# First attention: one VectorE instruction for two heads' maxima from four PSUM banks, and a scores' ring of two banks

## The chip, the cores and the metric

The kernel runs on one core of a Trainium2 chip. The metric is the device time of one execution in microseconds (us), the median of several. TensorE (PE) multiplies, its weight loader is listed apart (PEld); VectorE is DVE, ScalarE is ACT, GpSimd is POOL, and SyncE (SP) issues most of the DMAs. Results of TensorE go to PSUM, which has eight banks of 2 KB per partition; a bank holds 512 numbers of f32.

## What is computed

Two transformer layers over 2048 tokens of width 512: an attention with 16 heads of 32, a mixture of experts, an attention with one head of 512, and a gated MLP, each with a layer norm behind it. The change lies in the first attention:

```python
q = jnp.concatenate([q_sem, q_geo], axis=-1)
k = jnp.concatenate([k_sem, k_geo], axis=-1)
scores = jnp.einsum('bhqd,bhkd->bhqk', q, k).astype(jnp.float32) * scale
causal = jnp.tril(jnp.ones((S, S), dtype=bool))
scores = jnp.where(causal, scores, jnp.finfo(jnp.float32).min)
attn = jax.nn.softmax(scores, axis=-1).astype(v.dtype)
out = jnp.einsum('bhqk,bhkd->bhqd', attn, v)
```

## The kernel before

The program is a row of stages. `layer0_attention` is the second, after `layer0_qkv`, and all engines pass a border before the third (`layer0_project`) begins. In the trace it lies between about 152 and 731 us.

It works on 16 **items**, each one chunk c of 512 queries (c = 0 to 3) for a group of four heads. Items 0 to 3 have c = 0, items 4 to 7 c = 1, and so on. An item has 4(c+1) **steps**, one for each tile of 128 keys: 4 steps in each of items 0 to 3, 8 in 4 to 7, 12 in 8 to 11, 16 in 12 to 15, 160 in all. Scores are computed twice:

- **Maxima.** A softmax needs a maximum per query. For it TensorE multiplies 128 queries by up to 512 keys (line 866, a **unit**; 16(c+1) units in an item) into `sbank`, three banks used in turn (the **maxima's ring**). Most units are full, 128x512, and VectorE takes their maximum with one `reduce_max` (line 789, 384 of them). Units on the diagonal are 128 to 512 wide and go through an add with a mask and a maximum in one custom instruction (line 794, 256 of them). Heads are the innermost index: head 0, 1, 2, 3 of a query tile follow each other. When an item's maxima are complete, a **turn** transposes them on TensorE (line 873) into a bank of the same ring; ScalarE copies it out (line 758), and DMAs bring it into a row of the queries' tile. Units belong to an item some steps ahead of the one whose steps run.
- **Steps.** TensorE multiplies 128 keys by 512 queries, with the negated maximum as one more row (line 898; 895 and 900 at the diagonal), for each of four heads into `stb`, three banks used in turn (the **scores' ring**). ScalarE takes the exponential of each into `probs`, which has five slots (line 752). TensorE multiplies by the values (line 914), one step behind. GpSimd adds up the probabilities of four steps, in place, three adds in two halves each (line 711), and TensorE sums over the keys of that (line 930); VectorE turns and inverts it (lines 819 to 828), GpSimd multiplies (line 726).

The order of all this is one list (`attention0_plan`), and each engine runs through the list and takes its own events. In a step it reads: scores of head 0, units, head 1, units, head 2, units, values of the step before, sums if due, head 3, units. Mostly one unit stands behind each product of scores; in item 15, the last, none does. Before a unit, `free` waits until the bank's former content was reduced (`unit_max`); before a product of scores, TensorE waits until ScalarE is through with the product three before (`exp_ok`). TensorE, VectorE and ScalarE each take their work strictly in the list's order.

Of the kernel before, what the change touches and what calls it, by code (L numbers as in the profile page):

```python
# [18 lines left out]
ACT = mybir.ActivationFunctionType  # L19
AX = mybir.AxisListType.X  # L20
# [559 lines left out]
def layer0_attention(nc, stage_before, stored, landed, qx, qk_dram, m_dram, xs_dram, acc_dram, token, V, X, hi, lo, fifth, qst, consts, early, out_w, first_o):  # L580
    items, steps, first, final, units, loads, last_use, order = attention0_plan()
    unit_no, ring, scored = {}, {}, {}
    for at, ev in enumerate(order):
        if ev[0] == "unit":
            unit_no[ev] = len(unit_no)
        if ev[0] in ("unit", "turn"):
            ring[ev] = len(ring)
        if ev[0] == "scores":
            scored[ev[1], ev[2]] = at
    on_ring = sorted(ring, key=ring.get)  # L590
# [9 lines left out]
    with ExitStack() as ctx:  # L600
# [18 lines left out]
        stb = m.ps("stb", [P, 3, CH])  # L619
        sbank = m.ps("sbank", [P, 3, CH])  # L620
# [110 lines left out]
        def _(act):  # L731
            for ev in order:
                if ev[0] == "scores":
# [14 lines left out]
                    if per == 1:  # L748
                        to, got = probs[i % PSLOTS][:, h, w0:], stb[:, k % 3, w0:]
                    else:  # L750
                        to, got = probs[i % PSLOTS][:, h + 1 - per:h + 1, w0:], stb[:, k % 3, :].rearrange("p (h n) -> p h n", h=per)
                    nc.scalar.activation(to, got, ACT.Exp, scale=SCALE0).then_inc(s["exp_ok"], 1)  # L752
                elif ev[0] == "turn":
# [4 lines left out]
                    nc.scalar.activation(msb[:, n % 2, :], sbank[0:GH * TC, ring[ev] % 3, 0:P], ACT.Copy)\  # L758
# [78 lines left out]
        def _(pe):  # L837
            def free(ev):

                r = ring[ev]  # L840
                if r >= 3:
                    old = on_ring[r - 3]
                    if old[0] == "unit":
                        pe.wait_ge(s["unit_max"], unit_no[old] + 1)
                    else:
                        pe.wait_ge(s["mcopy"], old[1] + 1)
                return sbank[:, r % 3, :]

            fresh_q, fresh_k = set(range(EARLY)), set(range(EARLY))
            for ev in order:  # L850
# [23 lines left out]
                elif ev[0] == "scores":  # L874
# [10 lines left out]
                    if k >= 3 and j == 0:  # L885
                        pe.wait_ge(s["exp_ok"], k - 2)
# [3 lines left out]
                    if per > 1 and j == 0:  # L890
                        nc.tensor.matmul(stb[:, k % 3, :].rearrange("p (h n) -> p h n", h=per), identr[:],
                                         maskr[:, 0:wide].unsqueeze(1).broadcast_to([P, per, wide]), start=True, stop=False,
                                         skip_group_check=True)
                    if per > 1:
                        last = nc.tensor.matmul(stb[:, k % 3, j * wide:(j + 1) * wide], keys, asked, start=False, stop=j == per - 1,
                                                skip_group_check=True)
                    else:
                        last = nc.tensor.matmul(stb[:, k % 3, w0:], keys, asked, start=True, stop=kt < TC * c)  # L898
                        if kt >= TC * c:
                            last = nc.tensor.matmul(stb[:, k % 3, w0:w0 + P], identr[:], maskr[:, 0:P], start=False, stop=True)  # L900
# [1766 lines left out]
```

## Time and profile before

| | us |
|---|---|
| median of 3 runs | 2221.56 |
| the 3 runs | 2220.63, 2221.56, 2225.43 |
| the profiled execution | 2230.52 |
| its span, first to last instruction | 2228.7 |
| first attention, first unit to last sum, about | 152 to 731 |

The profile is of one execution, 9 us above the median. Its page gives busy times for each engine; stretches of the span can be asked for one by one. Two things need care. A busy PE is not a PE at its peak, since the records of neighbouring matmuls overlap: a product of 512 columns has a record of 0.40 us, and they start 0.235 us apart when nothing holds them. And a matmul that waits has its wait on the weight load in front of it, so a wait for a bank shows in the rows of PEld.

### The profile page before, as it was taken

What the parts mean: (1) busy time and instruction counts of PE and PEld (TensorE: products, weight loads), DVE (VectorE), ACT (ScalarE), POOL (GpSimd) and SP (SyncE); (2) the same over time, 40 slices, a digit from 0 to 9 for tenths busy, and PEclk for the clock granted to TensorE, in tenths of its full rate; (3) what the DMA queues carried; (4) which work ended last, traced back from release to release, by engine and by line L of the source; (5) the groups of instructions that cost most, each with busy time, mean ns of one, the idle gap of its engine ahead of it and who ended that gap; (6) DMA issues with size and microseconds to landing.
All of it is one profiled execution on the core that took longest, in us unless ns stands there. A gap on an engine that the chain in (4) does not pass through costs nothing. (4 is left out here: it accounts for less than half of the span.)

```text
span 2228.7 us, 27156 instructions
## 1 busy us (share of the span) xinstructions
PE 2130.8 (96%) x9788; PEld 1456.9 (65%) x9788; DVE 1190.0 (53%) x2306; ACT 736.7 (33%) x1264; POOL 824.5 (37%) x527
## 2 busy tenths in 40 slices
PE   7999999999997999999989999999999999999997
PEld 6875444444442654444467878888877888888886
DVE  5787777777762653222256633223246545564666
ACT  3324555555555322111144422111123211221123
POOL 4354889988999114432222340000003011212100
PEclk9988999999999999999999999999999999999999
DMA  5578355343310626555444360000101010100001
GB/s 180 182 199 191 93 125 139 96 96 72 72 32 18 252 101 230 131 99 92 79 146 141 133 217 29 19 19 29 38 1 57 1 38 20 38 19 28 10 19 57
DMA packets 104604, 197.24 MB, mean 89 GB/s; under 512 B 10384, under 2 KB 27664, under 8 KB 103056
## 3 DMA queue, kind: packets, MB, share of 16 engines
q1 hardware_dynamic: 92064, 162.78, 24.9%
q0 software_dynamic: 11408, 29.69, 5.9%
q10 hardware_dynamic: 1008, 3.15, 0.4%
q8 instruction: 75, 1.23, 0.2%
q14 instruction: 49, 0.40, 0.1%
HBM read 123.82 MB, written 71.75 MB: 88 GB/s over the span
## 5 line engine op out<-in xcount | busy, mean ns | idle before, releaser
L752 ACT ACTIVATE a_probs<-a_stb 128x512 f32<-128x512 f32 (+1 forms) x449 | 241.6, 587 | 189.8 <-PE a_stb L898 93.6
L2306 POOL CAST m_wh<-wst 128x1024 fp32r<-128x1024 f32 x24 | 26.6, 1108 | 719.4 <-POOLq L1591 369.2
L711 POOL TENSOR_TENSOR a_probs<-a_probs 128x1024 f32<-128x1024 f32 (+3 forms) x138 | 266.9, 1960 | 51.2 <-PE a_avb L914 35.7
L789 DVE TENSOR_REDUCE a_mparts<-a_sbank 128x1 f32<-128x512 f32 x384 | 240.4, 683 | 71.8 <-PE a_sbank L866 71.2
L57 PE MATMUL m_gu<-hi,m_wh 128*128 128x512 f32 x512 | 199.8, 390 | 3.0 <-DVE m_h L2436 1.6
L59 PE MATMUL m_gu<-hi,m_wl 128*128 128x512 f32 x512 | 199.4, 389 | 0.0
L58 PE MATMUL m_gu<-lo,m_wh 128*128 128x512 f32 x512 | 199.3, 389 | 0.0
L2385 DVE TENSOR_TENSOR m_h<-m_sg,m_gu 128x512 f32<-128x512 f32 x63 | 43.3, 687 | 191.6 <-ACT m_sg L2336 191.3
L794 DVE CUSTOM_DVE_ANT_0 a_junk<-a_sbank,hidden 128x128 bf16<-128x128 f32 (+3 forms) x256 | 113.7, 488 | 48.8 <-PE a_sbank L866 47.4
L866 PE MATMUL a_sbank<-hi,q 96*128 96x512 f32 (+3 forms) x320 | 121.5, 405 | 7.9 <-DVE a_mparts L789 3.2
L2336 ACT ACTIVATE m_sg<-m_gu 128x512 f32<-128x512 f32 x64 | 38.3, 598 | 261.3 <-PE m_gu L59 261.2
L914 PE MATMUL a_avb<-a_probs,V 128*32 128x512 f32 (+3 forms) x1024 | 122.6, 551 | 0.0
L2038 DVE TENSOR_TENSOR ptl<-q_tb,pth 128x512 fp32r<-128x512 f32 x64 | 44.0, 691 | 143.2 <-ACT pth L1887 143.2
L1887 ACT ACTIVATE pth<-q_tb 128x512 fp32r<-128x512 f32 x64 | 38.2, 598 | 245.2 <-PE q_tb L2165 245.2
L1362 POOL DMA_INDIRECT acc<-e_rows_b,X x37 | 57.8, 1563 | 164.6 <-DVE e_rows_b L1486 131.3
L866 PE MATMUL a_sbank<-lo,q 96*128 96x512 f32 (+3 forms) x272 | 107.9, 423 | 4.6 <-DVE a_mparts L789 4.3
L57 PEld LDWEIGHTS m_gu<-hi,m_wh 128*128 128x128 f32 x512 | 96.1, 188 | 23.6 <-DVE m_h L2436 2.0
L898 PE MATMUL a_stb<-q,hi 97*128 97x512 f32 (+1 forms) x256 | 109.6, 432 | 1.1 <-DMA q<-max 0.7
L59 PEld LDWEIGHTS m_gu<-hi,m_wl 128*128 128x128 f32 x512 | 96.1, 188 | 20.0
L58 PEld LDWEIGHTS m_gu<-lo,m_wh 128*128 128x128 f32 x512 | 96.2, 188 | 19.8
L57 PE MATMUL q_vb<-vh,pth 128*128 128x512 f32 x256 | 102.0, 398 | 3.2 <-DMA vl<-v 3.2
L57 PE MATMUL m_yb<-m_wh,m_hh 128*128 128x512 f32 x256 | 102.0, 398 | 2.8 <-DVE X L2389 2.7
(324 smaller groups left out, 4943.9 us busy)
## 6 DMA issues: line engine op xcount, KB each, us to landing
hi<-qk SPq DMA_DIRECT2D x66, 256.0 KB, 5.2
qk<-v_hl SPq DMA_DIRECT2D x32, 512.0 KB, 2.9
lo<-qk SPq DMA_DIRECT2D x54, 256.0 KB, 5.2
wst<-in_w_mlp SPq DMA_DIRECT2D x24, 512.0 KB, 3.5
q<-qk SPq DMA_DIRECT2D x42, 256.0 KB, 6.4
xs<-a_zeros POOLq DMA_DIRECT2D x39, 264.0 KB, 3.0
X<-xs SPq DMA_DIRECT2D x39, 264.0 KB, 2.7
v<-vhl SPq DMA_DIRECT2D x16, 512.0 KB, 4.0
```

The costliest lines, as they stand in the source:

```text
L57: nc.tensor.matmul(out, wh, xh, start=start, stop=False, skip_group_check=True)
L58: nc.tensor.matmul(out, wh, xl, start=False, stop=False, skip_group_check=True)
L59: return nc.tensor.matmul(out, wl, xh, start=False, stop=stop, skip_group_check=True)
L711: nc.gpsimd.tensor_tensor(probs[to % PSLOTS][:, hs, w0:], probs[to % PSLOTS][:, hs, w0:], probs[other % PSLOTS][:, hs, w0:], ALU.add)\
L752: nc.scalar.activation(to, got, ACT.Exp, scale=SCALE0).then_inc(s["exp_ok"], 1)
L789: nc.vector.reduce_max(to, sbank[:, b, :], AX).then_inc(s["unit_max"], 1)
L794: nc.vector.tensor_tensor_reduce(out=junk[:, k % 2, 0:w], in0=sbank[:, b, 0:w], in1=hidden[:, CH - w:CH], scale=1.0, scalar=BIG, op0=ALU.a ...
L866: nc.tensor.matmul(bank[:, 0:w], qs[q_slot[n]][0:96, h, t * P:(t + 1) * P], kst[at % KSLOTS][0:96, h, 0:w], start=True, stop=True)\
L898: last = nc.tensor.matmul(stb[:, k % 3, w0:], keys, asked, start=True, stop=kt < TC * c)
L914: last = nc.tensor.matmul(avb[HD0 * h:HD0 * (h + 1), w0:], V[:, kt, g * P + h * HD0:g * P + (h + 1) * HD0], probs[i % PSLOTS][:, h, w0:], ...
L1362: nc.gpsimd.indirect_dma_start(acc_dram[:, :], bass.IndirectOffsetOnAxis(ap=to[:, j:j + 1], axis=0), y[:, j % 2, :], None, compute_op=ALU. ...
L2038: nc.vector.tensor_tensor(ptl[:, 4 * g:4 * g + 4, :].rearrange("p a b -> p (a b)"), tb[:, (g + 1) % 2, :], f32(pth[:, 4 * g:4 * g + 4, :]) ...
```

## The change

All of it is in `layer0_attention`. VectorE no longer takes the maximum of each full unit: it skips the units of heads 0 and 2, and at those of heads 1 and 3 it takes the maxima of both heads with one `reduce_max` over two neighbouring banks, 128x2 out of 128x1024. So 384 instructions become 192; the 256 of the diagonal stay. For this the maxima's ring has four banks, and a turn takes two places of it, so that pairs begin at an even bank. Since PSUM has eight banks and two serve the values and the sums, the scores' ring keeps two: a product of scores now waits for the exponential of the product two before. In nine places a turn stands between the units of a pair; there the instruction reads the second bank of the turn's place, with an older unit in it, in place of the unit of head 0, which for those 128 queries and one head changes the number that is subtracted ahead of the exponential.

```diff
         if ev[0] in ("unit", "turn"):
-            ring[ev] = len(ring)
+            ring[ev] = len(on_ring)
+            on_ring += [ev] * (1 if ev[0] == "unit" else 2)
...
-        stb = m.ps("stb", [P, 3, CH])
-        sbank = m.ps("sbank", [P, 3, CH])
+        stb = m.ps("stb", [P, 2, CH])
+        sbank = m.ps("sbank", [P, 4, CH])
...
-                    k, b = unit_no[ev], ring[ev] % 3
+                    k, b = unit_no[ev], ring[ev] % 4
                     to = mparts[:, n % 2, h * TC + t, u:u + 1]
+                    if u < items[n][0] and h % 2 == 0:
+                        continue
                     dve.wait_ge(s["unit_ok"], k + 1)
                     if u < items[n][0]:
-                        nc.vector.reduce_max(to, sbank[:, b, :], AX).then_inc(s["unit_max"], 1)
+                        pair = mparts[:, n % 2, :, u].rearrange("p (h t) -> p h t", t=TC)[:, h - 1:h + 1, t]
+                        nc.vector.reduce_max(pair, sbank[:, b - 1:b + 1, :], AX).then_inc(s["unit_max"], 2)
...
-                if r >= 3:
-                    old = on_ring[r - 3]
+                if r >= 4:
+                    old = on_ring[r - 4]
...
-                    if k >= 3 and j == 0:
-                        pe.wait_ge(s["exp_ok"], k - 2)
+                    if k >= 2 and j == 0:
+                        pe.wait_ge(s["exp_ok"], k - 1)
```

Everywhere else `stb[:, k % 3` becomes `k % 2`, and `sbank`'s `% 3` becomes `% 4`.

TensorE's order is the same before and after; only what its waits ask for differs. One step with a sum, in item 14 of the kernel before (`a_stb` the scores' ring, `a_sbank` the maxima's, `a_avb` the values' bank, `a_den` the sums'):

```order
L898 MATMUL a_stb<-q,lo 128x512 [waits a0_exp_ok]
L866 MATMUL a_sbank<-hi,q 128x512 [waits a0_unit_max]
L898 MATMUL a_stb<-q,lo 128x512 [waits a0_exp_ok]
L866 MATMUL a_sbank<-hi,q 128x512 [waits a0_unit_max]
L898 MATMUL a_stb<-q,lo 128x512 [waits a0_exp_ok]
L866 MATMUL a_sbank<-hi,q 128x512 [waits a0_unit_max]
L914 MATMUL a_avb<-a_probs,V 32x512 [waits a0_exp_ok]
L914 MATMUL a_avb<-a_probs,V 32x512 x3
L930 MATMUL a_den<-a_probs,a_ones 32x512 [waits a0_sum_ok]
L930 MATMUL a_den<-a_probs,a_ones 32x512 x3
L898 MATMUL a_stb<-q,lo 128x512 [waits a0_exp_ok]
L866 MATMUL a_sbank<-hi,q 128x512 [waits a0_unit_max]
```

Every L898 and every L866 in it has a wait, so each can hold all that stands below it.

On VectorE, at the border of items 13 and 14 (`a_mparts` the maxima, `a_dt`, `a_rec`, `a_rt` the inverted sums), before:

```order
L789 TENSOR_REDUCE a_mparts<-a_sbank 128x1 [waits a0_unit_ok] x19
L819 STREAM_TRANSPOSE a_dt<-a_den 128x512 [waits a0_rec_ok,a0_den_ok]
L823 RECIPROCAL a_rec<-a_dt 128x16 [waits a0_rt_ok,a0_dt_ok]
L828 STREAM_TRANSPOSE a_rt<-a_rec 128x512 [waits a0_o_ok,a0_rec_ok]
L789 TENSOR_REDUCE a_mparts<-a_sbank 128x1 [waits a0_unit_ok] x29
```

and with the change:

```order
L792 TENSOR_REDUCE a_mparts<-a_sbank 128x2 [waits a0_unit_ok] x9
L822 STREAM_TRANSPOSE a_dt<-a_den 128x512 [waits a0_rec_ok,a0_den_ok]
L826 RECIPROCAL a_rec<-a_dt 128x16 [waits a0_rt_ok,a0_dt_ok]
L831 STREAM_TRANSPOSE a_rt<-a_rec 128x512 [waits a0_o_ok,a0_rec_ok]
L792 TENSOR_REDUCE a_mparts<-a_sbank 128x2 [waits a0_unit_ok] x15
```

The 48 maxima became 24 instructions, and the nineteenth, which stood ahead of the inversion, is now taken behind it, with the twentieth.

## Rows read from the trace of the kernel before

**Rows 1.** The page, part 1: busy us, share of the span, instructions.

```profile
PE 2130.8 (96%) x9788; PEld 1456.9 (65%) x9788; DVE 1190.0 (53%) x2306; ACT 736.7 (33%) x1264; POOL 824.5 (37%) x527
```

**Rows 2.** Stretches: length, busy PE, PEld, DVE, ACT, POOL (instructions), granted clock, DMA share, GB/s.

```profile
340.00:668.00 328.00, 316.31 (x1823) 155.53 (x1819) 236.58 (x532) 190.32 (x363) 304.27 (x168) 0.99 0.37 85
668.00:731.00 63.00, 48.81 (x272) 16.63 (x268) 16.99 (x10) 35.16 (x69) 53.44 (x26) 0.92 0.06 17
```

**Rows 3.** Waits, 340 to 668 us: who waited, for whom, us, times, longest.

```profile
POOL a_probs L711 <- PE a_avb L914: 20.0, 13, 2.5
...
PE a_sbank L866 <- DVE a_mparts L789: 5.2, 13, 0.8
...
PE a_den L930 <- POOL a_probs L711: 2.9, 4, 1.0
```

**Rows 4.** VectorE by shape, 340 to 668: count, busy us, mean ns, idle before.

```profile
L789 DVE TENSOR_REDUCE a_mparts<-a_sbank 128x1 f32<-128x512 f32 x280 | 175.0, 683 | 54.6 <-PE a_sbank L866 54.2
L794 DVE CUSTOM_DVE_ANT_0 a_junk<-a_sbank,hidden 128x512 bf16<-128x512 f32 x28 | 18.4, 688 | 6.9 <-PE a_sbank L866 6.6
...
L794 DVE CUSTOM_DVE_ANT_0 a_junk<-a_sbank,hidden 128x128 bf16<-128x128 f32 x28 | 7.5, 288 | 4.0 <-PE a_sbank L866 3.8
```

**Rows 5.** ScalarE by shape in the same stretch.

```profile
L752 ACT ACTIVATE a_probs<-a_stb 128x512 f32<-128x512 f32 x257 | 139.6, 600 | 93.5 <-PE a_stb L898 63.5 <-PE a_stb L895 18.6 <-PE a_stb L900 6.5
```

**Rows 6.** Timeline, a step of item 14: start us, length us, engine, line.

```profile
647.67 1.08 ACT L752 ACTIVATE a_probs<-a_stb 128x512 f32<-128x512 f32 x2 [0.32 <-PE a_stb L898]
...
647.94 0.19 PEld L898 LDWEIGHTS a_stb<-q,hi 97*128 97x128 f32 x1
...
648.17 0.40 PE L898 MATMUL a_stb<-q,hi 97*128 97x512 f32 x1
```

**Rows 7.** Timeline, the first of the 99 short steps.

```profile
227.74 1.60 ACT L752 ACTIVATE a_probs<-a_stb 128x512 f32<-128x512 f32 x3 [1.85 <-PE a_stb L895]
...
228.75 0.40 PE L898 MATMUL a_stb<-qx,hi 97*128 97x512 f32 x1
```

**Rows 8.** Timeline, the last of them.

```profile
665.59 0.96 PE L898 MATMUL a_stb<-q,hi 97*128 97x512 f32 x3
...
666.13 1.09 ACT L752 ACTIVATE a_probs<-a_stb 128x512 f32<-128x512 f32 x2 [2.04 <-PE a_stb L898]
```

**Rows 9.** Timeline in item 15, where products wait for exponentials.

```profile
712.57 4.72 POOL L711 TENSOR_TENSOR probs<-probs,a_probs 128x1024 f32<-128x1024 f32 x2 [0.27 <-PE a_avb L914]
...
715.00 0.53 PEld L898 LDWEIGHTS a_stb<-q,lo 97*128 97x128 f32 x3 [0.84 <-ACT a_probs L752]
...
715.54 1.57 ACT L752 ACTIVATE a_probs<-a_stb 128x512 f32<-128x512 f32 x3 [0.55 <-PE a_stb L898]
716.19 0.19 PEld L898 LDWEIGHTS a_stb<-q,lo 97*128 97x128 f32 x1 [0.66 <-ACT a_probs L752]
...
716.62 0.16 PEld L914 LDWEIGHTS a_avb<-a_probs,V 128*32 128x32 f32 x8 [0.24 <-issue]
```

**Rows 10.** Timeline at the border of items 13 and 14.

```profile
614.97 0.40 PE L866 MATMUL a_sbank<-lo,q 96*128 96x512 f32 x1
...
615.40 1.89 DVE L789 TENSOR_REDUCE a_mparts<-a_sbank 128x1 f32<-128x512 f32 x3 [0.57 <-PE a_sbank L866]
...
616.15 0.19 PEld L866 LDWEIGHTS a_sbank<-lo,q 96*128 96x128 f32 x1
616.38 0.39 PE L866 MATMUL a_sbank<-lo,q 96*128 96x512 f32 x1
```

**Rows 11.** Line 866 in the whole run: what its idle time ended with (us, times).

```profile
  DVE a_mparts L789: 25.7, 67
  DVE a_mparts L794: 16.2, 45
```

**Rows 12.** Timeline at the end of item 15.

```profile
721.98 0.16 PEld L930 LDWEIGHTS a_den<-probs,a_ones 128*32 128x32 f32 x8 [2.60 <-POOL probs L711]
...
727.67 1.90 PE L930 MATMUL a_den<-a_probs,a_ones 128*32 128x512 f32 x16
```

More of the change, by code:

```diff
@@ L581, in layer0_attention @@
     items, steps, first, final, units, loads, last_use, order = attention0_plan()
-    unit_no, ring, scored = {}, {}, {}
+    unit_no, ring, scored, on_ring = {}, {}, {}, []
     for at, ev in enumerate(order):
@@ L586, in layer0_attention @@
         if ev[0] in ("unit", "turn"):
-            ring[ev] = len(ring)
+            ring[ev] = len(on_ring)
+            on_ring += [ev] * (1 if ev[0] == "unit" else 2)
         if ev[0] == "scores":
             scored[ev[1], ev[2]] = at
-    on_ring = sorted(ring, key=ring.get)
     slot_of = {load: at for at, load in enumerate(loads)}
@@ L748, in _ @@
                     if per == 1:
-                        to, got = probs[i % PSLOTS][:, h, w0:], stb[:, k % 3, w0:]
+                        to, got = probs[i % PSLOTS][:, h, w0:], stb[:, k % 2, w0:]
                     else:
-                        to, got = probs[i % PSLOTS][:, h + 1 - per:h + 1, w0:], stb[:, k % 3, :].rearrange("p (h n) -> p h n", h=per)
+                        to, got = probs[i % PSLOTS][:, h + 1 - per:h + 1, w0:], stb[:, k % 2, :].rearrange("p (h n) -> p h n", h=per)
                     nc.scalar.activation(to, got, ACT.Exp, scale=SCALE0).then_inc(s["exp_ok"], 1)
@@ L757, in _ @@
                         act.wait_ge(s["mstore"], 16 * (n - 1))
-                    nc.scalar.activation(msb[:, n % 2, :], sbank[0:GH * TC, ring[ev] % 3, 0:P], ACT.Copy)\
+                    nc.scalar.activation(msb[:, n % 2, :], sbank[0:GH * TC, ring[ev] % 4, 0:P], ACT.Copy)\
                         .then_inc(s["mcopy"], 1)
@@ L846, in free @@
                         pe.wait_ge(s["mcopy"], old[1] + 1)
-                return sbank[:, r % 3, :]
+                return sbank[:, r % 4, :]
             fresh_q, fresh_k = set(range(EARLY)), set(range(EARLY))
@@ L890, in _ @@
                     if per > 1 and j == 0:
-                        nc.tensor.matmul(stb[:, k % 3, :].rearrange("p (h n) -> p h n", h=per), identr[:],
+                        nc.tensor.matmul(stb[:, k % 2, :].rearrange("p (h n) -> p h n", h=per), identr[:],
                                          maskr[:, 0:wide].unsqueeze(1).broadcast_to([P, per, wide]), start=True, stop=False,
@@ L894, in _ @@
                     if per > 1:
-                        last = nc.tensor.matmul(stb[:, k % 3, j * wide:(j + 1) * wide], keys, asked, start=False, stop=j == per - 1,
+                        last = nc.tensor.matmul(stb[:, k % 2, j * wide:(j + 1) * wide], keys, asked, start=False, stop=j == per - 1,
                                                 skip_group_check=True)
                     else:
-                        last = nc.tensor.matmul(stb[:, k % 3, w0:], keys, asked, start=True, stop=kt < TC * c)
+                        last = nc.tensor.matmul(stb[:, k % 2, w0:], keys, asked, start=True, stop=kt < TC * c)
                         if kt >= TC * c:
-                            last = nc.tensor.matmul(stb[:, k % 3, w0:w0 + P], identr[:], maskr[:, 0:P], start=False, stop=True)
+                            last = nc.tensor.matmul(stb[:, k % 2, w0:w0 + P], identr[:], maskr[:, 0:P], start=False, stop=True)
                     if j < per - 1:
```

## The prediction, made before the changed kernel was run

> **What bounds the kernel now.** The page first: PE is busy 96% of the span, VectorE 53%, ScalarE 33%, GpSimd 37% [rows 1]. The change lies in the first attention alone, so the second view is the busy time there, by stretch. Items 8 to 14, 340 to 668 us, have PE at 316 of 328 us, GpSimd at 304, VectorE at 237, ScalarE at 190 [rows 2]. Two engines are near the top, and the waits tell which leads: GpSimd waits 20.0 us for the values' product, TensorE waits 2.9 us for GpSimd at the sums and 5.2 us for VectorE's maxima [rows 3]. So TensorE's list sets the pace here, GpSimd follows with 7% to spare, and a delay put into TensorE's list mostly stays in the time. Item 15 is another regime: no units, PE busy 49 of 63 us, GpSimd 53 [rows 2]; there GpSimd leads. Nothing behind the stage overlaps it, so what the stage gains or loses, the kernel does.
>
> VectorE, whose work the change cuts, is not the bound: 237 of 328 us, and it sits idle 54.6 us ahead of its maxima because units aren't there yet [rows 2, 4].
>
> **VectorE's part.** A maximum of 512 columns takes 683 ns; the masked form takes 288 ns at 128 and 688 at 512 columns [rows 4], so (688 - 288) / 384 = 1.04 ns a column and some 155 ns beside. The trace has no reduction of 1024 columns out of two banks. Bounds: 1024 x 1.04 = 1065 ns with nothing beside, 2 x 683 = 1366 with nothing saved; I take 1065 + 155 = 1220, since both forms show that offset. Saved: 192 x (1366 - 1220) = 28 us of VectorE's time, of which none is on the path. What matters is the other end: a bank comes free up to 1.22 us after the second unit of a pair was written, where it was 0.68 after its own unit. The Trainium skill (Perfetto Trace Analysis, "Optimizing Scalar/DVE Operations") says that grouping into larger operations can improve throughput if the engine is saturated. By this rule the pairing would pay only where VectorE is full, and at 237 of 328 us it is not; the sum below would not move.
>
> **The scores' ring: the main term.** ScalarE's exponential of 512 columns takes 600 ns [rows 5]. With three banks a product waits for the exponential three back, which is long done. With two it waits for the one two back. I laid every product's recorded start beside the recorded end of the exponential two back. Take the last head of a step in item 14: its exponential starts at 647.67 and ends 0.60 later, at 648.27; the product two on has its weights loaded at 647.94 and starts at 648.17 [rows 6]. It would have to wait. What a wait costs is seen in item 15, where it happens today: the exponential that starts at 715.54 ends at 716.14, the weights are loaded at 716.19, 0.05 later, and the next work follows 716.62 - 716.19 = 0.43 us after, against some 0.33 where the weights lay ready [rows 9]. The load is thus no longer hidden: 0.05 + 0.10, say 0.16 us on top of the exponential's end. In rows 6 that is 648.27 + 0.16 - 648.17 = 0.26 us.
>
> Within a step the second and the third product can both be late, but a delay of the second serves the third as well, so one step costs the larger of the two; the exponential of the last head moves along with its product, so the next step pays again. Counted so, 99 of the 128 steps of items 4 to 14 come out short. The first is at 228.75, where the second exponential of the row ends at about 228.84 (starts are 0.5 apart): 0.25 us. The last is the third product of a run that began at 665.59, due at 666.15, against an exponential that ends at 666.73: 0.7 us [rows 7, 8]. Their sum is 24 us; with 0.06 in place of 0.16 it would be 15. Items 0 to 3 add 0.2. **Term: +24, bounds 15 and 24.**
>
> **The maxima's ring.** Four banks in pairs look deeper than three, but the distance from a unit to the reduction it waits for stays three units for the first of a pair, and the reduction is longer. Where the pair lies between scores without the values' product inside, TensorE gives VectorE over 2 us and nothing is short. In 65 of the 192 pairs the values' product stands between the halves; in 50 of these the bank is wanted again before the next values' product. One of them [rows 10]: the second half is written at 614.97, VectorE starts 0.43 later at 615.40 and would be done at 616.62, while the load for that bank stands at 616.15 and the unit at 616.38. The load would come at 616.67, the unit's work 0.42 us late. The scores' wait of that step has already taken 0.26 of it, so 0.16 is left: 50 x 0.16 = 8, less where two units lie together. At the low end VectorE's free time covers it (0), at the high end the waits do not merge (50 x 0.42 = 21). **Term: +7.** In return, today's waits on VectorE go where the fourth bank or the later scores cover them, 5.2 us in rows 3 and more in items 0 to 7, and those on GpSimd (2.9) go since GpSimd is less behind. Most of the 16.2 us that ended with a masked maximum [rows 11] lie ahead of the first step, where VectorE's own pace decides, and stay. **Term: -8**, bounds -12 and -3.
>
> **Item 15.** A step takes 2.6 us: its last product begins at 715.00, and the values of the next follow at 716.62, some 1.0 us ahead of the next last product [rows 9]. With two banks: the second product loads 0.54 + 0.60 + 0.05 = 1.19 us after the step's start, the third another 0.49 on (the pitch of exponentials), the values 0.43 behind, the next step 0.99 behind: 3.10. GpSimd needs 6 x 2.36 us for four steps (two halves in 4.72 [rows 9]), 3.5 us a step, so it hides nearly all while it is behind. Not hidden: the place where it caught up and waited 0.27 us for the values [rows 9], three steps after a border, some 1.5 us, and the last two steps, from 721.98, after the last wait for GpSimd, to 727.67 [rows 12], some 1. **Term: +3**, bounds 0 and 8.
>
> **Sum.** 24 + 7 - 8 + 3 = **+26 us**. On the profiled execution that is 2230.5 + 26 = 2256.5; the profile lies 9 us above the median, and the sum carries over: 2221.6 + 26 = **2248 us**.
>
> **The rivals.**
>
> *GpSimd takes it up.* If GpSimd and not TensorE leads in items 8 to 14, a TensorE that is some 8% slower only waits less. For it: 304 of 328 us busy. Against it: GpSimd's own 20 us of waiting for TensorE, which is most of its idle time [rows 2, 3]. Left would be item 15 and a little: +3, 2225.
>
> *Faster.* The four banks remove TensorE's waits on VectorE and two banks suffice for the scores. It decides if a held load is hidden after all, that is if the exponential's end may come 0.2 us after the recorded load without harm. Price: -5.2 in rows 3, and some 4 more in items 0 to 7: -9, 2212. Rows 6 to 8 speak against it: the exponential ends behind the product's recorded start.
>
> *The delays pile up.* The two rings' waits add instead of merging (15 more), and the clock falls. Item 15, where TensorE waits often, has a granted clock of 0.92, items 8 to 14 0.99 [rows 2]. If these had 0.92 as well, 316 us of PE work would take 316 x (0.99 / 0.92 - 1) = 24 us more: 2272, or 2287 with both. The Trainium skill (TensorE: Matmul & The Clock Gate, "A second HAM failure mode: psum-queue depth-cycling") tells of a kernel in which short idle times between groups of matmuls, as PSUM banks are cycled, made the clock swing between its two levels. The row of item 15 agrees in kind; in items 8 to 14 such idle times are few today.
>
> *The pair is no cheaper than two maxima*, 1366 ns: then each of the 50 places costs 0.15 more, +7, 2255.
>
> **How the numbers follow.** Forecast 62%; pile-up 20%; GpSimd takes it up 10%, a fifth of that above the border; faster 6%; no cheaper pair 2%. About 0.2%, 4.4 us, is what a measurement of this kernel can tell from no change. Faster 0.06, within it 0.08, slower 0.86. The range: low 2229, which leaves out the faster rival and most of the one with GpSimd; high 2272, the pile-up with either of its halves, which leaves out both together. The forecast's own bounds lie inside: 15 + 0 - 12 + 0 = +3 would need all four low at once; 15 + 4 - 10 + 1 = +10 and 24 + 14 - 4 + 6 = +40 are what I hold likely.
>
> **What would show it.** In the profile of the changed kernel: weight loads of `a_stb` idle until the exponential, in about 100 steps of items 4 to 14; 192 reductions of about 1.22 us; VectorE's busy time down some 28 us; GpSimd's wait for the values up; the stage's end later by the whole loss, and the stages behind it unchanged. If GpSimd's idle time stays at 20 us while TensorE waits for it, the first step was wrong; if loads don't wait for exponentials, the main term was.

## The result, and the profile after

The kernel after takes **2284.51 us** (median of 5 runs, 2282.51 to 2295.65), against 2225.43 for the kernel before, measured along with it: a ratio of 1.027, 95% interval 1.0248 to 1.0291. The change costs 59 us; the forecast was 26. The sign was right, the forecast size less than half of the measured one, and the time lies above the range.

The profiled execution took 2295.65 us, the longest of the five, with a span of 2293.9. The loss lies where it was expected. From the first start of each step's products and the end of the last sum in the records, the last sum of the first attention ends at 791.8 us, where it was 730.4; behind it follow 1502 us, before 1498. By items: 1 to 3 lost 7.3 us, 4 to 14 lost 49, item 15 lost 6.8.

The page of the kernel after, parts 1 and 5 (busy us, mean ns of one, idle time ahead and what ended it); they answer to [rows 1, 4, 11]:

```profile
PE 2180.5 (95%) x9788; PEld 1461.5 (64%) x9788; DVE 1180.1 (51%) x2114; ACT 747.7 (33%) x1264; POOL 824.5 (36%) x527
...
L792 DVE TENSOR_REDUCE a_mparts<-a_sbank 128x2 f32<-128x1024 f32 x192 | 230.8, 1222 | 127.3 <-PE a_sbank L869 126.8
...
L869 PE MATMUL a_sbank<-hi,q 96*128 96x512 f32 (+3 forms) x320 | 120.6, 406 | 18.9 <-DVE a_mparts L792 16.9
```

The paired reduction takes 1222 ns, as forecast (1220). PE has the same 9788 instructions and is busy 50 us longer, which is no more work: a matmul behind a wait has a record of 0.50 us, one in a row of 0.40 (timelines below), and some run at the lower clock.

Stretches of the kernel after: items 8 to 14, item 15, and two neighbouring 7 us of item 9 (columns as in [rows 2]):

```profile
358.00:723.00 365.00, 343.09 (x1824) 153.84 (x1821) 232.00 (x392) 197.18 (x363) 305.21 (x168) 0.97 0.33 76
723.00:792.00 69.00, 57.00 (x268) 18.38 (x267) 15.66 (x10) 36.70 (x68) 52.23 (x26) 0.83 0.05 14
422.00:429.00 7.00, 6.64 (x28) 3.23 (x28) 2.99 (x17) 1.74 (x3) 5.99 (x4) 0.53 0.07 27
429.00:436.00 7.00, 6.90 (x47) 3.34 (x43) 4.10 (x14) 2.97 (x6) 3.30 (x4) 0.99 0.32 93
```

Items 8 to 14 take 365 us in place of 328 with the same work: GpSimd is at 305 us, as it was at 304, so it has 60 us to spare where it had 24. The clock column matters too: 0.97 and 0.83, where [rows 2] have 0.99 and 0.92. The last two lines show what a fall looks like: granted 0.53, nearly all at the lower level (1.2 GHz), 28 matmuls in 7 us with PE "busy" 6.64; then 0.99 and 47 of them.

The waits in items 8 to 14 of the kernel after (who waited, for whom, us, times, longest), and below them those of the kernel before that [rows 3] don't show:

```profile
PEld a_stb L901 <- ACT a_probs L752: 54.2, 134, 0.9
POOL a_probs L711 <- PE a_avb L917: 46.4, 19, 4.4
...
PEld a_sbank L869 <- DVE a_mparts L792: 27.2, 42, 1.6
...
PE a_sbank L869 <- DVE a_mparts L792: 18.7, 29, 1.2
...
PEld a_den L933 <- POOL a_probs L711: 1.1, 3, 0.5
```

```profile
PEld a_stb L898 <- ACT a_probs L752: 23.9, 33, 0.8
...
PEld a_sbank L866 <- DVE a_mparts L789: 11.0, 29, 0.6
...
PEld a_den L930 <- POOL a_probs L711: 10.6, 14, 1.5
```

In the order of the forecast: loads for the scores wait for exponentials in 134 places, where they did in 33; GpSimd waits 46.4 us for TensorE (20.0 in [rows 3]), so it didn't take the loss up; the sums' wait for GpSimd is nearly gone (1.1 in place of 10.6). The line that was not forecast in this size is the one for VectorE's maxima: matmuls waited 5.2 us for them [rows 3], now 18.7, and their weight loads 11.0, now 27.2 (the two overlap and aren't to be added). VectorE is busy 232 of 365 us all the while, so it is late without being full.

### The profile page after: what moved, and what is told of

Read it like the earlier page. It is cut to its first block and busy times, and to the rows that moved or that the text cites. A ratio compares the mean times of both kernels' runs of the same rounds, so it can differ in the third digit from the quotient of the medians.

```text
span 2293.9 us, 27156 instructions
## 1 busy us (share of the span) xinstructions
PE 2180.5 (95%) x9788; PEld 1461.5 (64%) x9788; DVE 1180.1 (51%) x2114; ACT 747.7 (33%) x1264; POOL 824.5 (36%) x527
## 5 line engine op out<-in xcount | busy, mean ns | idle before, releaser
L752 ACT ACTIVATE a_probs<-a_stb 128x512 f32<-128x512 f32 (+1 forms) x449 | 250.0, 584 | 227.9 <-PE a_stb L901 110.5
L792 DVE TENSOR_REDUCE a_mparts<-a_sbank 128x2 f32<-128x1024 f32 x192 | 230.8, 1222 | 127.3 <-PE a_sbank L869 126.8
L917 PE MATMUL a_avb<-a_probs,V 128*32 128x512 f32 (+3 forms) x1024 | 129.2, 578 | 0.0
L901 PE MATMUL a_stb<-q,hi 97*128 97x512 f32 (+1 forms) x256 | 118.0, 462 | 3.9 <-ACT a_probs L752 1.5
L901 PE MATMUL a_stb<-q,lo 97*128 97x512 f32 (+1 forms) x224 | 103.2, 470 | 9.7 <-ACT probs L752 5.1
```

The source lines that it names most:

```text
L792: nc.vector.reduce_max(pair, sbank[:, b - 1:b + 1, :], AX).then_inc(s["unit_max"], 2)
L901: last = nc.tensor.matmul(stb[:, k % 2, w0:], keys, asked, start=True, stop=kt < TC * c)
L917: last = nc.tensor.matmul(avb[HD0 * h:HD0 * (h + 1), w0:], V[:, kt, g * P + h * HD0:g * P + (h + 1) * HD0], probs[i % PSLOTS][:, h, w0:], ...
```

## The experiments

In all of them the same stage was edited and the rest left alone. "Ratio" is to the kernel before, measured along with each run; differences in us are of the medians, and can be some 3 us off what the ratio gives. The first question was which half of the change costs the time: the scores' ring of two, or the pairs.

**E1, the scores' ring alone.** The kernel before, with two scores' banks; the maxima's ring keeps three, so one bank of PSUM is unused.

```diff
-        stb = m.ps("stb", [P, 3, CH])
+        stb = m.ps("stb", [P, 2, CH])
...
-                    if k >= 3 and j == 0:
-                        pe.wait_ge(s["exp_ok"], k - 2)
+                    if k >= 2 and j == 0:
+                        pe.wait_ge(s["exp_ok"], k - 1)
```

> Only the scores' ring is cut from three banks to two; the maxima's ring keeps three banks and VectorE takes each maximum by itself. One bank stays unused. Theory 'ring' (most of the 59 us comes from products of scores that wait for the exponential two back): 40 us or more over the kernel before, 2265 to 2280, with steps of items 12 to 14 longer by 0.26 us where no values' product stands in a pair and by the same 0.26 where one does. Theory 'pairs' (most comes from banks that come free only after the second unit of a pair): the ring alone costs the 24 us counted beforehand and some 5 in item 15, 2250 to 2257; the steps that grew by 0.48 us grow by 0.26 only, and those with a turn (+1.3 and +3.0 us) by 0.3 or less.

Measured: 2242.94, ratio 1.0064 (1.0045 to 1.0084), so +17, less than either theory said. **E2, four banks without pairs.** E1 with the maxima's ring of four; every unit has its own reduction and its own release, and a turn takes one place:

```diff
-        sbank = m.ps("sbank", [P, 3, CH])
+        sbank = m.ps("sbank", [P, 4, CH])
...
-                if r >= 3:
-                    old = on_ring[r - 3]
+                if r >= 4:
+                    old = on_ring[r - 4]
```

> Scores' ring of two banks, maxima's ring of four, each maximum by itself and each bank released by itself, a turn in one place. Against the first of this call it tells what the fourth bank alone gives, against the changed kernel what the pairing costs. Both theories: TensorE's waits for maxima nearly gone (under 3 us in items 8 to 14, where the kernel before has 5), 3 to 10 us less than with three banks. Theory 'ring': only 10 to 15 us under the changed kernel, 2268 to 2275. Theory 'pairs': 30 us or more under it, 2240 to 2255.

Measured: 2230.14, ratio 1.0011 (0.9993 to 1.0028): +4, which this measurement cannot tell from nothing, and again less than either theory said. So everything the change does to PSUM, without the pairs, is as good as free, and **the pairs**, with the turn's second place that they ask for, **cost 2284.5 - 2230.1 = 54 us**. The waits of E1 (340 to 680 us), then of E2 (336 to 664), about their items 8 to 14:

```profile
PEld a_stb L898 <- ACT a_probs L752: 58.3, 138, 0.9
...
PEld a_den L930 <- POOL a_probs L711: 4.0, 13, 0.4
PE a_sbank L866 <- DVE a_mparts L789: 4.0, 13, 0.6
```

```profile
PEld a_stb L898 <- ACT a_probs L752: 64.7, 150, 0.9
...
PEld a_den L930 <- POOL a_probs L711: 6.9, 16, 1.1
...
PE a_den L930 <- POOL a_probs L711: 1.2, 3, 0.7
...
PE a_sbank L866 <- DVE a_mparts L789: 0.7, 3, 0.3
```

Both have all the waits for exponentials that the kernel after has (134 times there), and E2 is no slower for it. What E2 doesn't have is the wait for maxima: 0.7 us in place of 18.7.

Step by step one sees where the price of the scores' ring goes. Durations of single steps, from the start of their first product to that of the next step (us, worked out from the records; items 12 and 13):

| step | what it holds | before | E1 | E2 | after |
|---|---|---|---|---|---|
| 104 | units, no values' product in a pair | 2.43 | 2.68 | 2.66 | 2.68 |
| 105 | the same | 3.06 | 3.34 | 3.33 | 3.33 |
| 106 | with a sum | 3.92 | 4.18 | 4.19 | 4.19 |
| 111 | values' product inside a pair | 3.06 | 3.33 | 3.33 | 3.56 |
| 110 | a turn, inside a pair in after | 4.65 | 4.66 | 4.54 | 7.62 |
| 126 | a turn, inside a pair in after | 4.67 | 4.66 | 4.56 | 5.96 |
| 115 | units of an item's border | 3.70 | 3.69 | 3.20 | 4.24 |
| 118 | with a sum, GpSimd behind | 4.49 | 3.77 | 4.21 | 4.06 |

The price of a typical step is near the 0.26 us forecast: 0.25 to 0.28 in E1's steps 104 to 106. But at step 118 E1 takes 0.72 us less than before: there a matmul of the sums stood waiting 0.78 us for GpSimd (at 584.33 us of the kernel before), and in E1 only the weight load of the sums waits, 0.21 us. At item borders the fourth bank gives more back (step 115, E2).

**E3, is it the wide instruction or the late release?** The kernel after, with two reductions of 512 columns behind the second unit in place of one of 1024, and the same joint release:

```diff
-                        pair = mparts[:, n % 2, :, u].rearrange("p (h t) -> p h t", t=TC)[:, h - 1:h + 1, t]
-                        nc.vector.reduce_max(pair, sbank[:, b - 1:b + 1, :], AX).then_inc(s["unit_max"], 2)
+                        for d in (1, 0):
+                            one = mparts[:, n % 2, (h - d) * TC + t, u:u + 1]
+                            last = nc.vector.reduce_max(one, sbank[:, b - d, :], AX)
+                        last.then_inc(s["unit_max"], 2)
```

> The changed kernel, but VectorE takes the two maxima of a pair with two instructions, first head first, and gives both banks back after the second. VectorE has 28 us more to do, and starts no earlier. If the joint release and the late start are what costs, it is the changed kernel again, 0 to +8 us (2284 to 2293), with steps with the values' product inside a pair longer by 0.05 to 0.1 more. If it is the wide instruction itself (two banks read at once while TensorE writes a third), it is faster by 5 us or more.

Measured: 2284.58, ratio 1.0251 (1.0215 to 1.0287); the kernel after, as far as one can tell (that the medians agree to a tenth is luck, the four runs lie between 2279 and 2287). The instruction as such is innocent: what is left is that VectorE begins only when the second unit is there, and that it frees both banks at the end; E11 takes these two apart. E3 also shows how little the pair saves. In items 8 to 14 of the kernel after, and from 350 to 706 us of E3 (by shape: count, busy us, mean ns):

```profile
L792 DVE TENSOR_REDUCE a_mparts<-a_sbank 128x2 f32<-128x1024 f32 x140 | 168.2, 1222 | 88.1 <-PE a_sbank L869 87.8
```

```profile
L793 DVE TENSOR_REDUCE a_mparts<-a_sbank 128x1 f32<-128x512 f32 x286 | 178.9, 683 | 85.9 <-PE a_sbank L871 85.3
```

A single has a record of 683 ns, but the records of neighbours overlap, so that a single adds 178.9 / 286 = 626 ns of busy time. Two are 1.25 us, the pair is 168.2 / 140 = 1.20.

**E4, a fixed order.** To keep the values' product out of every pair: scores of heads 0 and 1, then all units of the step in whole pairs, scores of heads 2 and 3, values, sums.

```diff
-            if h == 3 and i > 0:
-                order.append(("av", i - 1))
...
+        order += [("scores", i, 0), ("scores", i, 1)] + rows[i] + [("scores", i, 2), ("scores", i, 3)]
+        if i > 0:
+            order.append(("av", i - 1))
```

> The changed kernel with another order within a step: scores of heads 0 and 1, then all the step's units, whole pairs only, a turn never inside a pair, then scores of heads 2 and 3, then values and sums. Two products that share a bank now have the units or the values' product between them: by the durations of the trace the third product comes 1.4 us after the first, against 1.29 that a full wait asks for, and pairs have at least 1.2 us. If waits on the two rings are the whole cause, with the clock's falls following from them, the time goes back to that of the kernel before or below, 2205 to 2235, item 15 keeping a loss of 3 to 7. If something else in the pairing costs (VectorE's reads of two banks, the fewer banks for the scores in diagonal steps), 2250 or more stays.

Measured: 2263.09, ratio 1.0145 (1.0107 to 1.0183). Some 21 us came back, far less than the theory of the waits expected (2205 to 2235). The run moved too many things at once: with its units in a row TensorE may come back to a pair's bank sooner (not shown), and its matmuls still wait 12.4 us for maxima in items 8 to 14, 11 times, now up to 1.5 us. It doesn't tell how much the torn pairs cost; the next two do.

**E5 and E6, torn pairs made whole.** The kernel after, where only the first unit of a torn pair is moved, directly ahead of its mate. E6 does it for the nine pairs with a turn inside (`to == at + 2`), E5 also for those with the values' product inside:

```diff
+        to = at + 1 + (flat[at + 1][1][0] == "turn")
+        if to == at + 2 or (k + 1) // 4 != (flat[to][0] + 1) // 4:
+            in_gap[k].remove(ev)
+            home = in_gap[flat[to][0]]
+            home.insert(home.index(flat[to][1]), ev)
```

> The changed kernel, but only the turns are moved: where one stood inside a pair (9 places), the first unit of the pair is moved behind it. Theory 'torn pairs': the steps with a turn, 15 us longer than with single maxima, fall by about 1 us each in 9 places and the clock stays up there, 10 to 18 us back, 2266 to 2275. If the turn's two places cost and not its place inside the pair, the same steps stay as they are, 2280 to 2287.

> The changed kernel, but wherever a turn or a values' product stood between the two units of a pair, the first unit is moved behind it, next to the second. Rings and instructions are those of the change. Theory 'torn pairs' (a bank whose unit waits for its mate holds TensorE; 24 us in the steps with the values' product inside, 16 in those with a turn, the rest from falls of the clock that follow): 30 to 45 us back, 2235 to 2255. Theory 'long reduction' (1.22 us from two banks is too long for the ring wherever it stands): at most 15 us back, 2268 or more.

Measured: E6 2267.41, ratio 1.0191 (1.017 to 1.0213), E5 2250.46, ratio 1.0112 (1.0092 to 1.0133). Both lie where the theory of torn pairs put them. So of the 54 us nine turns cost **17**, the values' product inside pairs another **17**, and 20 stay with whole pairs; with four or five runs each, a part is uncertain by some 7 us. Step 110 falls from 7.62 us to 4.84 in both, step 111 from 3.56 to 3.55 in E6 and 3.31 in E5. Over the stage of the profiled runs, the steps with a turn inside a pair and the steps right behind them take 16 us less in E6 than in the kernel after, and the other steps with the values' product inside a pair 14 us less in E5 than in E6. The waits of E6, then of E5, in items 8 to 14:

```profile
PE a_sbank L879 <- DVE a_mparts L802: 14.1, 25, 1.2
```

```profile
PE a_sbank L879 <- DVE a_mparts L802: 6.7, 12, 1.1
```

What a turn does is read from the timeline of the kernel after, step 110 (start us, length us, engine, line):

```profile
597.56 0.28 PE L876 MATMUL a_sbank<-ident,a_nm 128*16 128x128 f32 x1
...
597.59 0.48 PE L869 MATMUL a_sbank<-hi,q 96*128 96x512 f32 x1
...
598.17 1.23 DVE L792 TENSOR_REDUCE a_mparts<-a_sbank 128x2 f32<-128x1024 f32 x1 [0.67 <-PE a_sbank L869]
...
599.45 0.19 PEld L869 LDWEIGHTS a_sbank<-hi,q 96*128 96x128 f32 x1 [1.59 <-DVE a_mparts L792]
599.45 0.50 PE L869 MATMUL a_sbank<-hi,q 96*128 96x512 f32 x1 [1.16 <-DVE a_mparts L792]
```

The turn (first line) takes two of the ring's four places. So the very next unit behind the pair's second half (second line) needs a bank of the pair that was only just written: TensorE stands still from 598.3 to 599.4, for the whole paired reduction. And the same step as [rows 10], where the values' product stood inside a pair, in the kernel after:

```profile
666.34 0.40 PE L869 MATMUL a_sbank<-lo,q 96*128 96x512 f32 x1
...
666.85 2.41 DVE L792 TENSOR_REDUCE a_mparts<-a_sbank 128x2 f32<-128x1024 f32 x2 [1.12 <-PE a_sbank L869]
667.19 0.19 PEld L901 LDWEIGHTS a_stb<-q,hi 97*128 97x128 f32 x1 [0.41 <-ACT a_probs L752]
...
668.13 0.19 PEld L869 LDWEIGHTS a_sbank<-lo,q 96*128 96x128 f32 x1 [0.27 <-DVE a_mparts L792]
668.13 0.50 PE L869 MATMUL a_sbank<-lo,q 96*128 96x512 f32 x1
```

VectorE begins 0.51 us behind the second unit, ends at 668.07, and the load follows 0.06 later: the wait of 0.27 us comes on top of those for the exponentials (0.41) of the same step. It isn't merged away by them.

**E8, the length alone.** The kernel after, reading 256 of the 512 columns of either bank (half of the keys are left out of those maxima), everything else as in after:

```diff
-                        nc.vector.reduce_max(pair, sbank[:, b - 1:b + 1, :], AX).then_inc(s["unit_max"], 2)
+                        nc.vector.reduce_max(pair, sbank[:, b - 1:b + 1, 0:CH // 2], AX).then_inc(s["unit_max"], 2)
```

> The changed kernel, but each paired reduction reads only the first 256 of the 512 columns of both banks, so the other half of the keys is left out of those maxima. Order, rings and the joint release stay; the instruction takes 0.155 + 512 x 1.04 = 0.69 us in place of 1.22, about what a single maximum took. If the length of the reduction is what counts, all but the scores' ring comes back: 2225 to 2245. If the joint release is (the first unit's bank is held until the second unit is there, however short the reduction), 2262 or more stays.

Measured: 2245.03, ratio 1.0094 (1.0075 to 1.0114). That is the upper end of what "the length counts" had allowed. The reduction now takes 690 ns (344 to 675 us of E8):

```profile
L792 DVE TENSOR_REDUCE a_mparts<-a_sbank 128x2 f32<-128x512 f32 x136 | 93.3, 690 | 133.4 <-PE a_sbank L869 132.9
```

0.53 us less between the second unit and the release give back 39 of the 54 us, with all torn pairs in place. **E11, the same without leaving anything out**: the rings, the order and the joint release of the kernel after, but the first unit is reduced as soon as it is there:

```diff
+                    dve.wait_ge(s["unit_ok"], k + 1)
                     if u < items[n][0] and h % 2 == 0:
+                        nc.vector.reduce_max(to, sbank[:, b, :], AX)
                         continue
...
-                        nc.vector.reduce_max(pair, sbank[:, b - 1:b + 1, :], AX).then_inc(s["unit_max"], 2)
+                        nc.vector.reduce_max(to, sbank[:, b, :], AX).then_inc(s["unit_max"], 2)
```

> Rings, order and the joint release of the changed kernel, but two reductions of one bank each: the first is taken as soon as its unit is there, the second as soon as its own is, and both banks come free with the second. What stands between a pair's second unit and the release is 0.68 us as with single maxima, not 1.22. If the wait for the whole reduction behind the second unit is what costs, it comes near the half-width reductions, 2235 to 2252; if the joint release alone holds TensorE (a first unit's bank is kept until its mate is there, 1 us later and more where a turn or the values' product lies between), 2262 or more.

Measured: 2253.67, ratio 1.0112 (1.0074 to 1.015). 31 us come back, although VectorE has a little more to do than in the kernel after; 24 us over E2 stay, with the joint release and the turns' two places. This lies between the two theories, nearer to the first. The Trainium skill (Perfetto Trace Analysis, "Optimizing Scalar/DVE Operations") has the rule that fits: where VectorE isn't saturated but leaves bubbles on another engine, breaking up instructions may let the work end sooner. E11 agrees, with 31 us; E3, broken up but started no earlier, gained nothing, so it is the early start that counts.

**E12, whole pairs and half the width**, E5 and E8 together:

```diff
-                        nc.vector.reduce_max(pair, sbank[:, b - 1:b + 1, :], AX).then_inc(s["unit_max"], 2)
+                        nc.vector.reduce_max(pair, sbank[:, b - 1:b + 1, 0:CH // 2], AX).then_inc(s["unit_max"], 2)
```

> Whole pairs (no turn and no values' product inside, as in the run with moved first units) together with reductions of 256 of the 512 columns of both banks; the maxima leave out half of the keys. If torn pairs and the length of the reduction are the two parts of what pairing costs, and add up to it, nothing is left over single maxima with four banks: 2226 to 2238. If a third thing costs (pairs as such, or the two places of a turn), 2243 or more.

Measured: 2235.01, ratio 1.0033 (1.0015 to 1.0051), 5 us above E2. With the pair short and its halves together, the 54 us are down to 5, as expected if these two parts are all. The waits of E8, E11 and E12 for maxima in items 8 to 14, in this order:

```profile
PE a_sbank L869 <- DVE a_mparts L792: 6.0, 16, 0.6
```

```profile
PE a_sbank L869 <- DVE a_mparts L792: 7.4, 17, 0.9
```

```profile
PE a_sbank L879 <- DVE a_mparts L802: 1.7, 5, 0.6
```

Beside the medians this row makes one series over the kernels with two scores' banks and four maxima's banks, which is a strong sign that the wait for maxima is the cause. (It counts items 8 to 14 of one execution, the medians the whole; the last column is span x (1 - mean granted clock), the mean over all runs of a kernel, an estimate of the full-clock time that was not granted.)

| kernel | PE waits for maxima, us | median us | clock not granted, us |
|---|---|---|---|
| E2 | 0.7 | 2230 | 39 |
| E12 | 1.7 | 2235 | 41 |
| E8 | 6.0 | 2245 | 44 |
| E5 | 6.7 | 2250 | 50 |
| E11 | 7.4 | 2254 | 49 |
| E4 | 12.4 | 2263 | 54 |
| E6 | 14.1 | 2267 | 46 |
| after | 18.7 | 2285 | 58 |
| E3 | 19.6 | 2285 | 52 |

The waits are smaller than the losses, since the row covers little more than half of the stage: over all of it, 152 to 800 us, it has 31.2 us in the kernel after and 1.5 in E2.

**Can something be won from it?** E2 leaves a kernel with short steps that pays 0.26 us in each for the scores' ring. **E7** takes that away: E2, with the units that stood behind the third product moved ahead, so that the exponential has longer:

```diff
+        three = [ev for gap in in_gap[k:k + 3] for ev in gap]
+        first_two = (2 * len(three) + 2) // 3
+        in_gap[k], in_gap[k + 1], in_gap[k + 2] = three[:first_two], three[first_two:], []
```

> Scores' ring of two banks, maxima's ring of four, single maxima and single releases, and of the units that stand behind the first three products of a step two thirds now stand behind the first, the rest behind the second, none behind the third. By the durations of the trace the second product then comes 1.29 us after the last of the step before, and the third 1.7: neither waits. The waits of 0.26 us a step (99 steps) go: 10 to 20 us under the same rings in the old order (2230), so 2208 to 2220, under the kernel before. If the waits for exponentials were not what the ring of two costs, no change: 2225 to 2235.

Measured: 2228.39, ratio 1.0016 (1.0004 to 1.0029). Nothing gained, although it does what it says: steps 104 to 106 are back at 2.43, 3.11 and 3.96. But step 114, with a sum, grows from 4.17 to 4.88. The waits of E7, 336 to 664 us, against 6.9 and 1.2 in E2 above:

```profile
PEld a_den L934 <- POOL a_probs L715: 11.7, 13, 1.8
...
PE a_den L934 <- POOL a_probs L715: 5.1, 4, 1.3
```

TensorE now reaches the sums before GpSimd does. It seems that GpSimd's adds set a floor right under the time of the kernel before, but no run shows it. **E9 and E10** tried to lower that floor: the multiplication by the inverted sums (line 726) goes from GpSimd to VectorE for every item, E9 on top of E7, E10 on the kernel before.

```diff
-                    if n == NI - 1:
+                    if n >= 0:
                         dve.wait_ge(s["avs_ok"], n + 1)
                         dve.wait_ge(s["rt_ok"], n + 1)
-                        nc.vector.tensor_tensor(X[:, n, :], avs[:, n % 2, :], rt[:, n % 2, :], ALU.mult).then_inc(s["o_ok"], 1)
+                        nc.vector.tensor_tensor(X[:, items[n][0] * NG + items[n][1], :], avs[:, n % 2, :], rt[:, n % 2, :], ALU.mult).then_inc(s["o_ok"], 1)
```

> The run with moved units (two scores' banks, four maxima's banks, single maxima), and the multiplication of the values by the inverted sums, 1.28 us on GpSimd for each of 15 items, goes to VectorE (0.69 us there, in the trace of the kernel before for the last item). There steps of 3.33 us fell to 3.11 but steps with a sum grew to 4.5 to 4.9, waiting for GpSimd. If GpSimd is what took the gain, it falls by half to all of the 15 x 1.28 = 19 us: 2208 to 2219, under the kernel before. If not, no change: 2224 to 2232.

> The kernel before with that multiplication on VectorE, as a control of the last one. TensorE's own list is the longest there and GpSimd is waited for 2.9 us in items 8 to 14: a gain of 2 to 10 us, 2215 to 2223, most of it in item 15, where GpSimd leads.

Measured: E9 2286.40, ratio 1.0257 (1.0227 to 1.0287), E10 2267.43, ratio 1.0193 (1.0163 to 1.0223). Both went the other way, E9 by 58 us against E7, E10 by 41 against the kernel before. VectorE takes its work in the list's order, so the multiplication stands ahead of maxima that TensorE wants. From E10: one line's instructions (min/median/max ns), a place in the timeline, and a wait in 340 to 700 us:

```profile
L834 DVE TENSOR_TENSOR X<-a_avs,a_rt x16: 692/1922/2611, 194.6 to 766.5; 128x512 f32<-128x512 f32 x16
```

```profile
403.94 4.68 POOL L711 TENSOR_TENSOR a_probs<-a_probs 128x1024 f32<-128x1024 f32 x2
...
406.59 2.59 DVE L834 TENSOR_TENSOR X<-a_avs,a_rt 128x512 f32<-128x512 f32 x1
...
409.11 0.68 DVE L789 TENSOR_REDUCE a_mparts<-a_sbank 128x1 f32<-128x512 f32 x1
```

```profile
PE a_sbank L866 <- DVE a_mparts L789: 19.9, 12, 3.5
```

The multiplication takes up to 2.6 us where 0.7 was expected, and TensorE waits 19.9 us for the maxima behind it (5.2 in [rows 3]): by another road the same kind of wait as in the kernel after. How much of the loss is the wait and how much the clock stays open. Reckoned as in the table, E10 lacks 70 us of clock and E9 81, the kernel before 38 and E7 44, so at most 32 of the 41 us and 37 of the 58 are the clock's. Nor do the two runs tell whether GpSimd sets a floor. No version was faster than the kernel before.

## Where the prediction was right, and which step failed

**The bound, right.** TensorE's list sets the pace, VectorE isn't the bound, what the stage loses the kernel loses. GpSimd's wait grew from 20.0 to 46.4 us instead of taking the loss up.

**VectorE's part: the instruction right, the saving wrong.** 1222 ns against 1220. But the 28 us that VectorE should be spared are 10: 230.8 us busy for 192 pairs, against 240.4 for 384 singles on the page of before:

```profile
L789 DVE TENSOR_REDUCE a_mparts<-a_sbank 128x1 f32<-128x512 f32 x384 | 240.4, 683 | 71.8 <-PE a_sbank L866 71.2
```

The saving was worked out from two records of 683 ns as 1366. They overlap when they follow each other, as could have been read from [rows 4] (175.0 / 280 = 625 ns each) and [rows 10] (three in 1.89 us, so 0.60 apart). The Trainium skill (Perfetto Trace Analysis, "Optimizing Scalar/DVE Operations") says of an instruction's data-access overhead that its profiled latency holds about twice the busy time, since the half for the write's acknowledgement overlaps with the next instruction; these rows agree in kind, with some 80 ns of overlap. By the same rows the rival "no cheaper" was nearly true of the engine's time, but not of the release.

**The scores' ring: local price right, sum wrong.** 0.26 us a step was forecast, 0.25 to 0.28 measured (steps 104 to 106). That an exponential three back is "long done" was not so everywhere: 33 loads waited for one in items 8 to 14 of the kernel before, 23.9 us. Of the sum, +24, a part was given back where TensorE would have waited for GpSimd anyway: E1 lost 17 in the median, in items 4 to 14 of its profile 10. The rival "GpSimd takes it up" was right for a part of this term: the loads of the sums waited 10.6 us for GpSimd, in E1 4.0. The 7% to spare that were read from [rows 2] say nothing of the sums' steps, where GpSimd is late already.

**The relief and item 15.** The fourth bank was worth 13 us (E1 to E2), forecast 8 for all relief; the waits for masked maxima, which were to stay mostly at 16.2 us [rows 11], are 6.8 in E2. In E2 item 15 lost 1.8 us, forecast 3. The 6.8 us that it lost in the profile of the kernel after are mostly not the ring's: in E3, with the same rings, it lost 1.0. The granted clock stood at the lower level for 24 us of item 15 there, for 10 in E3 and in the kernel before. All but the pairs was to be +19 and is +4.

**The maxima's ring: the step that failed.** Forecast +7, bounds 0 and 21; measured 54 (E2 to the kernel after). Three things went wrong in it.
- *The turn's two places were not priced.* The step counted distances in units; a turn takes half of the ring, so the next unit waits for a pair just written (1.16 us at 599.45). Nine such pairs, 17 us by E6. That a turn takes two places and stands inside nine pairs was in the change's text and needed no trace.
- *The waits merge less than assumed.* Of 0.42 us late in each of 50 places 0.26 were taken as served by the scores' wait, which left 0.16 each and 8 us (by the prediction's own 0.16 for a held load it is 616.62 + 0.16 - 616.38 = 0.40 us late, a trifle less). Step 111 shows 0.27 for the scores and 0.23 more for the pair; moving these pairs together gave 17 us (14 in the steps themselves), between the 8 and the 21 without any merging.
- *Whole pairs cost too*, 20 us (E5 against E2), which the step put at zero because "TensorE gives VectorE over 2 us". Where units come in bursts it doesn't: step 107 takes 4.36 us in E5, 3.84 with half the width (E12), 3.63 in E2. Halving the reduction removes 15 of the 20. By the table at most 50 - 39 = 11 of the 20 are the clock's.

**The rival that came nearest** was the pile-up with both of its halves, 2287, which the range left out. Its mechanism holds in part: the waits add in part, and the clock falls. But it spread a clock of 0.92 over items 8 to 14, where 0.97 was measured, and its 15 us for the addition know nothing of turns and whole pairs, 37 of the 54. That its time is so near is luck.

**What stays open: the clock's share.** E3 and the kernel after have the same waits and medians. Yet in the profiled runs item 9 took 46.0 us in E3, with no half-clock stretch in it, and 49.0 in the kernel after, which had 6.8 us of it (the stretch at 422). In E5, 22 of the 27 us that its profiled stage is longer than E2's lie in the items 2, 4, 5, 9, 10 and 15, and in each of these the clock fell (in E2 in item 15 alone, for a shorter time). But the bursts that wait are in these items too. By the table's last column the kernel after lacks 58 - 39 = 19 us of clock more than E2, so at most 19 of the 54 are the clock's, an upper estimate, since a low clock costs nothing while TensorE waits. E3's profiled run narrows it: its stage is 52 us longer than E2's, with 58 us at the lower level against 34, so at most half of the difference, 12 of the 52, is the clock's there. The falls come where TensorE waits in bursts; no run held the waits and changed the clock alone, so that the one causes the other was argued, not shown. In items 8 to 14 the sum comes out about right: 35 us longer than E2 (365 against 330), 18.0 of it in the row of waits, up to 365 x 0.03 = 11 at the lower clock, and 42 loads that are no longer hidden, at the 0.16 us of the forecast another 7.

## What to carry to other kernels

A ring of buffers is as deep as the time from a buffer's write to its release allows, not as its number: four banks freed in pairs served worse than three freed singly, and the engine that was "spared" had never been full. Before instructions are joined, go through the order for everything that may stand inside a pair or take two places of the ring, and price each; waits on different rings in one step should not be taken to merge unless a trace shows it. And a saving of an engine's time is read from its busy time over a run of neighbours, not from the records' lengths.

## What the runs showed of the hardware

- A VectorE maximum over two banks of PSUM, 128x1024 f32, takes 1222 ns, 128x512 out of two banks 690 ns, and out of one 683. Neighbouring reductions of 512 start some 600 ns apart (three in 1.89 us), so that their records overlap by some 80 ns.
- A VectorE multiplication 128x512 of two f32 operands in SBUF takes 0.69 us at best and up to 2.6 us beside GpSimd's add; at 406.59 above it ends 0.56 us behind the end of that add, near 408.62. In E10 all six multiplications with no add of GpSimd beside them took 0.69 us. The Trainium skill (SBUF — State Buffer, "Who interferes with whom") says that an instruction of VectorE with two inputs in SBUF contends with a GpSimd instruction that reads SBUF, and that this contention is an exclusive lock; the row agrees, since the rest of the add and one multiplication together make about that length.
- Behind the stage's first 30 us, of which every profiled run spent 24 to 27 at the lower level, the granted clock stood there for 68 us in the kernel after, for 20 in the kernel before and 10 in E2. In 7 us with such a stretch 28 matmuls ran, in the next 7 us, at the higher level, 47.
